# A decoder layer on one core: the fourth head's scores between two halves of the output projection, and unread matmuls in TensorE's waits

## The chip, the cores and the metric

The kernel runs on one core of a Trainium2 chip. The time is device microseconds (us) of one execution. A batch here means one of the 8 sequences, and a seam is the place where TensorE goes from one batch's last work to the next batch's.

## The reference, cut to what matters

For each of 8 sequences (512 tokens, 256 features, a context of 1024 tokens) the layer computes three blocks, each with a residual and a layer norm:

```python
x = layernorm(x + attn(x))            # convolution, position, qkv; 16 heads in bf16, 512 x 512 scores
y = causal_attention(x) + attention(x, ctx)     # 16 heads, fp32; 512 x 512 and 512 x 1024 scores
x = layernorm(x + y @ Wp + bp)
x = layernorm(x + routed_ffn(x))      # router, chosen expert, spline; then a norm of its own inside
```

The product `y @ Wp` of 512 x 256 by 256 x 256 in fp32 is the output projection of the title.

## The kernel before, in words

Five engines run hand-written streams that meet through semaphores. TensorE (PE) works its stream in order; nothing can be reordered by a scheduler.

A batch `b` on PE has two large stages. In the first, the heads stage, the 16 heads of the first attention are scored: `scores1(h)` writes four 128x512 tiles into banks 0 to 3 (line 1320), each after VectorE (DVE) has read the tile of the head before (semaphore `s1_evac`); `pv1(h)` multiplies by the values (line 1333). Heads 0 and 1 are scored at the end of the batch before (line 1304), so the loop at line 1394 begins with head 2, and "the fourth head" is `h == 3`. DVE scales every tile and takes its row minimum (line 768), ScalarE (ACT) takes the exponential (line 602), and both normalize (lines 961 and 612). In the second stage, 16 head groups of causal and cross attention are scored twice (lines 1501, 1505, 1540, 1543) and multiplied by the values (line 1558).

The seam carries the rest of the batch before (`c = b - 1`) between the heads of batch `b`:

- DVE ends batch `c` with `finish` (lines 1067 to 1073): `y_tmp`, which frees a slot (`slot_out`), then `y_sb` (`y_done`).
- PE waits for that slot, scores head 2, transposes `y_sb` (`heads_to_features`, line 1253), waits for ACT's copy `featA` (line 558), and runs the whole projection (`second_out`: `token_out` over 4 token tiles, line 1208, operands `wp_sb,featA`) into banks 5 and 6. `wp_mm` is raised once per two tiles.
- DVE's order is: norm of head 0, tiles of head 2, norm of head 1, tiles of head 3, then `second_residual` (lines 798, 773, 777: add banks 5 and 6 to `x_res`, sums of the norm), norm of head 2, `add_position` (line 752, writes `xs` of batch `b + 1`), tiles of head 4, `second_norm` (line 782, writes `r_sb`), norm of head 3, tiles of head 5.
- PE goes on with head 3, `position` (operands `xs,pe_sb`), head 4, then `first_qk` (`qk_sb,xs`), which waits for `add_position`, then head 5, `pv1(0)`, and the transposes of `r_sb`, whose copy `featB` ACT makes before its exponentials of head 5.

`keep_clock(at, n)` (line 1356) issues `n` bf16 matmuls of 128x512 into a bank that nobody reads; before the change it stands at the batch's end (4 of them) and four times later in the heads stage. `FILLERS` is 8. The last batch has no batch `b + 1` to prepare, and after it `tail` does the rest of the last sequence.

Of the kernel before, what the change touches and what calls it, by code (L numbers as in the profile page):

```python
# [37 lines left out]
def decoder_layer(nc, x, xT, ctxT, conv_w, peT, qkT, vT, outT, Wk, bk, Wq, bq, Wv, bv, Wck, bck, Wcq, bcq,  # L38
# [12 lines left out]
    NT = S // P  # L51
# [37 lines left out]
    FILLERS = 8  # L89
# [25 lines left out]
    with ctx:  # L115
        def sb(name, shape, dt=fp32):
            return ctx.enter_context(nc.sbuf_tensor(name, shape, dt))

        def sem(name):
            return ctx.enter_context(nc.semaphore(name))  # L120
# [8 lines left out]
        wp_sb = sb("wp_sb", [P, KD, D])  # L129
# [126 lines left out]
        out_mm, res_done, wp_mm = sem("out_mm"), sem("res_done"), sem("wp_mm")  # L256
        ln_stats, ln_var_in, ln_rstd, ln_done = ([sem(f"{n}{k}") for k in range(4)] for n in ("ln_stats", "ln_var", "ln_rstd", "ln_done"))
# [3 lines left out]
        slot_in, slot_out = sem("slot_in"), sem("slot_out")  # L261
# [103 lines left out]
        def uses_before(b, prev):  # L365
            return b * USES - FFN_USES if prev else 0
# [834 lines left out]
        def _(pe):  # L1201
# [3 lines left out]
            def project(dst, lhsT, rhs, tiles=KD):  # L1205

                for k in range(tiles):
                    last = mm(dst, lhsT(k), rhs(k), start=(k == 0), stop=(k == tiles - 1))  # L1208
                return last
# [12 lines left out]
            def position(b, m):  # L1222
                pe.wait_ge(conv_done, FIRST + b * KD + KD)
                project(bank[:, EXTRA_BANKS[m], :], lambda k: pe_sb[:, k, P * m:P * (m + 1)],
                        lambda k: xs[:, k, :]).then_inc(ex_mm, 1)

            def first_qk(b, i):

                if i == 0:
                    pe.wait_ge(ex_evac, (b + 1) * KD)  # L1230
                project(bank[:, EXTRA_BANKS[QK_AT[i]], :], lambda k: xs[:, k, P * i:P * (i + 1)], lambda k: qk_sb[:, k, :]).then_inc(ex_mm, 1)
# [7 lines left out]
                                       lambda k: v_sb[:, k, :])  # L1239
                    last.then_inc(ex_mm, 1)  # L1240

            def token_out(w, first_bank, done):

                for t in range(NT):
                    last = project(bank[:, first_bank + t // 2, D * (t % 2):D * (t % 2 + 1)], lambda k: featA[:, k, P * t:P * (t + 1)],
                                   lambda k: w[:, k, :])
                    if t % 2:
                        last.then_inc(done, 1)

            def to_features(src, first_bank, done):  # L1250
                for t in range(NT):
                    for k in range(KD):
                        last = nc.tensor.transpose(bank[:, first_bank + k, P * t:P * (t + 1)], src[:, t, P * k:P * (k + 1)], ident[:])
                last.then_inc(done, 1)

            def heads_to_features(c):
                pe.wait_ge(y_done, (c + 1) * HG)
                to_features(y_sb, 5, y_tr)

            def second_out(c):  # L1260
                pe.wait_ge(y_evac, c * 2 + 1)
                token_out(wp_sb, 5, wp_mm)

            def tokens_to_features(c):
                pe.wait_ge(ln_done[1], (c + 1) * NT)
                to_features(r_sb, 5, y_tr)

            def route(c):
                pe.wait_ge(y_evac, c * 2 + 2)
                for t in range(NT):  # L1270
                    last = project(bank[:, 7, ST * t:ST * (t + 1)], lambda k: featB[:, k, P * t:P * (t + 1)], lambda k: sigT[:, k, :])
                last.then_inc(route_mm, 1)

            def hidden_features(c):
                project(bank[0:HID, 5, :], lambda k: cw1_sb[:, k, :], lambda k: featB[:, k, :]).then_inc(gelu_in, 1)
# [36 lines left out]
            def batch(b, prev=True, ahead=True):  # L1312
                uses, base, c = all_uses[prev], uses_before(b, prev), b - 1

                def scores1(h):
                    i, rows = h // GH, slice(GW * (h % GH), GW * (h % GH + 1))
                    for t in range(NT):
                        n = NT * h + t
                        pe.wait_ge(s1_evac, b * H * NT + n - A1_BANKS + 1)
                        mm(bank[:, n % A1_BANKS, :], q_1[rows, i, P * t:P * (t + 1)], k_1[rows, i, :], start=True, stop=True,  # L1320
                           tile_position=(GW * (h % GH), 0)).then_inc(s1_mm, 1)

                def pv1(h):

                    if h < BY_DMA:
                        pe.wait_ge(p1T_in[h % E1_SLOTS], transposed(b, h))
                    else:
                        n = b * (H - BY_DMA) + h - BY_DMA
                        pe.wait_ge(tile_dve, n + 1)
                        pe.wait_ge(tile_act, n + 1)  # L1330
                    g = h // 2 % 4
                    for j in range(4):
                        last = mm(bank[GW * g:GW * (g + 1), PV1_BANKS[h // 8], :], v1[:, h, j, :], p1T[:, h % E1_SLOTS, :, j, :],  # L1333
                                  start=(h % 2 == 0 and j == 0), stop=(h % 2 == 1 and j == 3), tile_position=(0, GW * g))
                    last.then_inc(o1_mm, 1)
# [19 lines left out]
                    for _ in range(n):  # L1355
                        mm(bank[:, at, :], identb[:], k_1[:, 0, :], start=True, stop=True)

                if prev:
                    pe.wait_ge(slot_out, base)
                pe.wait_ge(qk_ready, (b + 1) * NT * 2)  # L1360
                pe.wait_ge(v1_ready, b * 16 + 16)
                def values(i):
                    if i == 0:
                        pe.wait_ge(ctx_in, b * 16 + 16)
                        if prev:
                            pe.wait_ge(tiles_in, b)
                        if ahead:
                            pe.wait_ge(qk_cast, (b + 1) * NT + 1)
                    else:
                        pe.wait_ge(vj_evac, b * PAIRS + i)  # L1370
                    if i == CTX_PAIRS and ahead:
                        pe.wait_ge(qk_cast, (b + 2) * NT)
                    if i == CTX_PAIRS + 1 and prev:
                        pe.wait_ge(spline_done, b)
                    for half in range(2):
                        dst = bank[:, 7 if i < CTX_PAIRS else VALUES_BANK, D * half:D * (half + 1)]
                        if i < CTX_PAIRS:
                            t = 2 * i + half
                            last = mm(dst, ctx_sb[:, P * t:P * (t + 1)], wcv_sb[:], start=True, stop=True)
                        else:  # L1380
                            t = 2 * (i - CTX_PAIRS) + half
                            last = project(dst, lambda k: featB[:, k, P * t:P * (t + 1)], lambda k: wv_sb[:, k, :])
                    last.then_inc(vj_mm, 1)
# [10 lines left out]
                for h in range(2, H):  # L1394
                    scores1(h)
                    if prev and h == 2:
                        heads_to_features(c)
                        second_out(c)
                    if h >= 5:
                        pv1(h - 5)  # L1400
                    if ahead and h == 3:
                        for m in range(KD):
                            position(b + 1, m)
                    if ahead and h == 4:
                        first_qk(b + 1, 0)
                        pe.wait_ge(ex_evac, (b + 2) * KD)
                    if prev:
                        if h == 5:
                            tokens_to_features(c)
                        if h == 6:  # L1410
                            if ahead:
                                pe.wait_ge(qk_cast, (b + 1) * NT + 1)
                            route(c)
                        if h == 7:
                            hidden_features(c)
                    if h in (8, 10, 12, 14):
                        values((h - 8) // 2)
                    if h in (9, 11, 13, 15):
                        context_key((h - 9) // 2)
                    if 9 <= h < 13:  # L1420
                        keep_clock(6, 4 if h % 2 else 2)
# [201 lines left out]
            def tail(c):  # L1623
                base = uses_before(c + 1, True)
                pe.wait_ge(slot_out, base)
                heads_to_features(c)
                second_out(c)
                tokens_to_features(c)
                route(c)
                hidden_features(c)  # L1630
                compressed(c)
                expert_columns(c, base, tail_uses)
                gather(c, base, tail_uses)
# [63 lines left out]
```

## Time and profile before

| what | us |
|---|---|
| runs | 2385.14, 2398.91, 2401.06 (median 2398.91) |
| the profiled execution | 2390.6 |
| its span | 2388.9 |
| TensorE busy | 2205.1 (92% of the span) |
| VectorE busy | 1876.4 (79%) |
| ScalarE busy | 1406.9 (59%) |

Matmul ends in the profile are modelled, so a busy PE is not PE at its peak. A row of the timeline merges neighbouring instructions of one kind; what stands in brackets is the idle time of the engine ahead of it and what ended that. The granted clock is given as a share of full speed: 1.00 is 2.4 GHz, 0.50 is 1.2 GHz.

### The profile page before, as it was taken

The page shows a single profiled execution, that of the slowest core. Times are in us where ns is not written, and L with a number is a line of the kernel's source. Part 1 is how long each engine was busy: PE and PEld are TensorE (multiplying, and loading weights), DVE is VectorE, ACT ScalarE, POOL GpSimd, SP SyncE. Part 2 cuts the span into 40 slices and gives each one's busy share as a digit, 9 for nine tenths or more (in the row PEclk, how much of TensorE's full clock was granted, in tenths as well). Part 3 has the DMA queues.
Part 4 walks back from the last instruction along what each step waited for, and adds up shares of the span by engine and source line. Part 5 has one row for each costly group of instructions (what it writes and reads, how often), then busy time and mean ns, then how long its engine had stood idle before and what let it go on. Part 6 is the DMA issues. An engine that isn't in the chain of part 4 may idle for free.

```text
span 2388.9 us, 37143 instructions
## 1 busy us (share of the span) xinstructions
PE 2205.1 (92%) x12850; PEld 1006.5 (42%) x12866; DVE 1876.4 (79%) x5149; ACT 1406.9 (59%) x2977; POOL 189.1 (8%) x349
## 2 busy tenths in 40 slices
PE   4999989999899998999989998999989999889992
PEld 1345433543345433454335443454334543345432
DVE  5868769788797879888698887988879786878854
ACT  2844678446764578546784466844677456754550
POOL 3011000100011000110001100010001100001000
PEclk8799999999999999999999998999989999789995
DMA  3600025000430006100160002500043000510000
GB/s 102 129 10 1 1 48 95 10 1 1 94 57 10 1 19 112 25 7 1 36 115 10 1 1 55 97 10 1 1 80 62 10 1 10 98 36 1 1 10 9
DMA packets 250843, 81.65 MB, mean 34 GB/s; under 512 B 236064, under 2 KB 247328, under 8 KB 250656
## 3 DMA queue, kind: packets, MB, share of 16 engines
q1 hardware_dynamic: 250656, 79.29, 16.3%
q8 instruction: 102, 1.67, 0.3%
q14 instruction: 85, 0.70, 0.1%
HBM read 16.35 MB, written 4.19 MB: 9 GB/s over the span
## 4 chain that ended last, share of the span: by engine, by line
PE 75%; ACT 11%; DVE 9%; issue 3%; DMA 1%; SPq 0%; POOL 0%; DVEq 0%; POOLq 0%; ACTq 0%
PE bank L1505 22%; PE bank L1558 13%; PE bank L1543 8%; PE bank L1208 7%; ACT work L602 6%; PE bank L1501 5%; PE bank L1460 4%; PE bank L1540 4%; DVE work L768 3%; PE bank L1333 2%; PE bank L1518 2%; ACT o1T L623 2%; PE bank L1320 1%; PE bank L1569 1%; ACT work L658 1%
## 5 line engine op out<-in xcount | busy, mean ns | idle before, releaser
L658 ACT ACTIVATE work<-bank 128x512 f32<-128x512 f32 (+3 forms) x1536 | 737.5, 553 | 561.6 <-PE bank L1543 287.2
L1037 DVE TENSOR_REDUCE top_half<-bank 128x1 f32<-128x512 f32 x1024 | 625.7, 682 | 24.1 <-PE bank L1505 24.1
L1505 PE MATMUL bank<-k_c,q_c 32*128 32x512 f32 x2048 | 630.7, 636 | 0.0
L1543 PE MATMUL bank<-q_c,k_c 32*128 32x512 f32 x2048 | 549.1, 629 | 0.0
L602 ACT ACTIVATE work<-work,neg 128x512 bf16<-128x512 bf16 x512 | 362.8, 718 | 60.7 <-DVE work L768 60.7
L768 DVE TENSOR_SCALAR_CACHE_REDUCE work<-bank 128x512 bf16<-128x512 f32 x512 | 322.4, 687 | 75.4 <-PE bank L1320 43.0
L1505 PEld LDWEIGHTS bank<-k_c,q_c 32*128 32x128 f32 x2048 | 274.5, 185 | 244.5 <-DVE top_half L1037 158.9
L1558 PE MATMUL bank<-work,v_flat 128*32 128x512 f32 (+3 forms) x3072 | 315.3, 545 | 9.2 <-ACT work L658 8.8
L1543 PEld LDWEIGHTS bank<-q_c,k_c 32*128 32x128 f32 x2048 | 227.0, 183 | 92.4 <-ACT work L658 57.2
L1034 DVE CUSTOM_DVE_ANT_0 masked<-bank,mask_w 128x384 bf16<-128x384 f32 (+3 forms) x512 | 223.1, 488 | 53.8 <-PE bank L1501 48.6
L1540 PE MATMUL bank<-q_s,k_s 32*128 32x512 f32 (+3 forms) x1024 | 259.1, 476 | 0.0
L1501 PE MATMUL bank<-k_s,q_s 32*128 32x128 f32 (+3 forms) x1024 | 198.5, 480 | 2.0 <-DVE top_s L1034 1.2
L1558 PEld LDWEIGHTS bank<-work,v_flat 128*32 128x32 f32 x3072 | 91.2, 109 | 234.4 <-issue 130.0
L1320 PE MATMUL bank<-k,q 32*128 32x512 bf16 x448 | 138.1, 401 | 26.6 <-DVE work L768 15.0
L1540 PEld LDWEIGHTS bank<-q_s,k_s 32*128 32x128 f32 x1024 | 141.6, 187 | 23.7 <-issue 8.9
L1333 PE MATMUL bank<-work,v 128*32 128x512 bf16 x512 | 145.2, 413 | 6.1 <-DMA work<-work 5.7
L1501 PEld LDWEIGHTS bank<-k_s,q_s 32*128 32x128 f32 x1024 | 102.9, 186 | 80.6 <-DVE top_s L1034 33.9
L517 POOL TENSOR_SCALAR ln_var<-mv 128x4 f32<-128x4 f32 x32 | 8.7, 272 | 1561.2 <-DVE mv L777 1561.2
L528 POOL TENSOR_SCALAR_AFFINE_SELECT work<-work 128x512 f32<-128x512 f32 x128 | 81.2, 634 | 602.8 <-ACT work L658 602.8
L1049 DVE COPY featA<-bank 128x512 f32<-128x512 f32 x64 | 44.3, 692 | 105.4 <-PE bank L1558 105.4
L961 DVE TENSOR_SCALAR work<-work,rden 128x512 bf16<-128x512 bf16 x424 | 123.0, 350 | 4.5
L602 ACT ACTIVATION_READ_ACCUMULATOR work<-work,neg 128x1 bf16 x512 | 102.3, 200 | 0.0
(191 smaller groups left out, 2260.4 us busy)
## 6 DMA issues: line engine op xcount, KB each, us to landing
xT_pad<-xT SPq DMA_DIRECT2D x16, 256.0 KB, 3.2
ctx_sb<-ctxT SPq DMA_DIRECT2D x8, 512.0 KB, 3.2
x_res<-x SPq DMA_DIRECT2D x8, 512.0 KB, 4.4
out<-r_sb SPq DMA_DIRECT2D x8, 512.0 KB, 3.1
work<-work SPq DMA_TRANSPOSE x112, 4.4
qk_sb<-qkT SPq DMA_DIRECT2D x1, 512.0 KB, 4.7
pe_sb<-peT SPq DMA_DIRECT2D x1, 256.0 KB, 4.4
v_sb<-vT SPq DMA_DIRECT2D x1, 256.0 KB, 5.5
```

Of the source, the lines that this page charges most:

```text
L602: nc.scalar.activation(e1[:, h % E1_SLOTS, t, :], s1[:, h % 2, t, :], ACT.Exp, bias=neg1[:, h % 2, t:t + 1], scale=-1.0, accum_out=den1[:, ...
L658: nc.scalar.activation(pT[:, s % PT_SLOTS, g, q0:S], exp_bank(n)[:, 0:S - q0], ACT.Exp, scale=SCALE).then_inc(pT_ready, 1)
L768: nc.vector.tensor_scalar(s1[:, h % 2, t, :], bank[:, (NT * h + t) % A1_BANKS, :], -SCALE, None, ALU.mult, ALU.min, accum_out=neg1[:, h % ...
L1034: nc.vector.tensor_tensor_reduce(masked[:, g, 0:n], scores[:, 0:n], mask_w[:, S - n:S], -1.0, -MASKED, ALU.add, ALU.min, top_s[:, i % 2, u ...
L1037: nc.vector.tensor_reduce(top_half[:, i % 2, g, u // 2, u % 2:u % 2 + 1], scores, AX.X, ALU.max, negate=True).then_inc(slot_out, 1)
L1208: last = mm(dst, lhsT(k), rhs(k), start=(k == 0), stop=(k == tiles - 1))
L1333: last = mm(bank[GW * g:GW * (g + 1), PV1_BANKS[h // 8], :], v1[:, h, j, :], p1T[:, h % E1_SLOTS, :, j, :], start=(h % 2 == 0 and j == 0), ...
L1501: mm(dst[:, 0:n], q_s[rows, i, P * u:n], k_s[rows, i, 0:n], start=True, stop=True, tile_position=(GW * g, 0)).then_inc(slot_in, 1)
L1505: mm(dst, q_c[rows, i, P * t:P * (t + 1)], k_c[rows, i, S * half:S * (half + 1)], start=True, stop=True, tile_position=(GW * g, 0)).then_i ...
L1540: mm(dst[:, 0:S - q0], k_s[rows, i, q0:q0 + P], q_s[rows, i, q0:S], start=True, stop=True, tile_position=(GW * g, 0)).then_inc(sT_mm, 1)
L1543: mm(dst, k_c[rows, i, P * u:P * (u + 1)], q_c[rows, i, :], start=True, stop=True, tile_position=(GW * g, 0)).then_inc(sT_mm, 1)
L1558: last = mm(dst[GW * g:GW * (g + 1), q0:S], v_flat[:, at:at + GW], pT[:, s % PT_SLOTS, g, q0:S], start=(s % BURST == 0), stop=(s % BURST = ...
```

## The change

Four edits, all on PE, all between the batches. The wait for `slot_out` moves from ahead of head 2 to behind it, with eight unread matmuls into bank 4 in between. Five more stand between the transposes of `y_sb` and the projection. The projection is cut in two: token tiles 0 and 1 ahead of `scores1(3)`, tiles 2 and 3 behind it. And where there is a next batch, eight unread matmuls into bank 6 stand ahead of `first_qk`, behind a wait until DVE has read bank 6 (`ln_stats[1]`). No other engine's stream is touched. The tail only calls the two halves one after the other.

```diff
-            def token_out(w, first_bank, done):
+            def token_out(w, first_bank, done, tiles):
-                for t in range(NT):
+                for t in tiles:
...
-            def second_out(c):
+            def second_out(c, half):
                 pe.wait_ge(y_evac, c * 2 + 1)
-                token_out(wp_sb, 5, wp_mm)
+                token_out(wp_sb, 5, wp_mm, range(2 * half, 2 * half + 2))
...
-                if prev:
-                    pe.wait_ge(slot_out, base)
                 pe.wait_ge(qk_ready, (b + 1) * NT * 2)
...
                 for h in range(2, H):
                     scores1(h)
                     if prev and h == 2:
+                        keep_clock(4, FILLERS)
+                        pe.wait_ge(slot_out, base)
                         heads_to_features(c)
-                        second_out(c)
+                        keep_clock(4, FILLERS // 2 + 1)
+                        second_out(c, 0)
+                    if prev and h == 3:
+                        second_out(c, 1)
                     if h >= 5:
                         pv1(h - 5)
                     if ahead and h == 3:
                         for m in range(KD):
                             position(b + 1, m)
                     if ahead and h == 4:
+                        if prev:
+                            pe.wait_ge(ln_stats[1], b * NT)
+                            keep_clock(6, FILLERS)
                         first_qk(b + 1, 0)
```

PE's stream at the first seam (batch 0 to batch 1), before the change, from the last transposes of batch 0 to the scores of head 5; `k,q` is a head's scoring, `k,identb` the unread matmuls:

```order
L1569 MATMUL bank<-ident,featA 128x128 x4
L1356 MATMUL bank<-k,identb 128x512 x4
L1320 MATMUL bank<-k,q 128x512 x4
L1253 MATMUL bank<-ident,y_sb 128x128 x8
L1208 MATMUL bank<-wp_sb,featA 128x256 x8
L1320 MATMUL bank<-k,q 128x512 x4
L1208 MATMUL bank<-xs,pe_sb 128x512 x4
L1320 MATMUL bank<-k,q 128x512 x4
L1208 MATMUL bank<-qk_sb,xs 128x512 x2
L1320 MATMUL bank<-k,q 128x512 x4
```

The same piece of PE's stream in the changed kernel, from the unread matmuls at the batch's end on:

```order
L1356 MATMUL bank<-k,identb 128x512 x4
L1320 MATMUL bank<-k,q 128x512 x4
L1356 MATMUL bank<-k,identb 128x512 x8
L1253 MATMUL bank<-ident,y_sb 128x128 x8
L1356 MATMUL bank<-k,identb 128x512 x5
L1208 MATMUL bank<-wp_sb,featA 128x256 x4
L1320 MATMUL bank<-k,q 128x512 x4
L1208 MATMUL bank<-wp_sb,featA 128x256 x4
L1208 MATMUL bank<-xs,pe_sb 128x512 x4
L1320 MATMUL bank<-k,q 128x512 x4
L1356 MATMUL bank<-k,identb 128x512 x8
L1208 MATMUL bank<-qk_sb,xs 128x512 x2
```

The scores of head 3 moved up past four of the projection's eight matmuls, and 21 unread matmuls came in at three places.

## Rows read from the trace of the kernel before

**Rows 1.** The page: span, TensorE's busy share, granted clock in 40 slices.
```profile
span 2388.9 us, 37143 instructions
PE 2205.1 (92%) x12850; PEld 1006.5 (42%) x12866; DVE 1876.4 (79%) x5149; ACT 1406.9 (59%) x2977; POOL 189.1 (8%) x349
PEclk8799999999999999999999998999989999789995
```

**Rows 2.** Chain that ended last, first seam: start us, us, what.
```profile
333.69 1.02 ACT featA L558
334.75 5.41 PE bank L1208 x16
...
348.58 3.63 PE bank L1208 x4
```

**Rows 3.** Timeline of PE, first seam: start us, us, group, idle before.
```profile
329.31 0.81 PE L1356 MATMUL bank<-k,identb 128*128 128x512 bf16 x3
331.59 1.03 PE L1320 MATMUL bank<-k,q 32*128 32x512 bf16 x4 [1.47 <-DVE y_tmp L1069]
332.56 1.09 PE L1253 MATMUL bank<-ident,y_sb 128*128 128x128 f32 x8
334.75 5.41 PE L1208 MATMUL bank<-wp_sb,featA 128*128 128x256 f32 x16 [1.10 <-ACT featA L558]
340.09 1.03 PE L1320 MATMUL bank<-k,q 32*128 32x512 bf16 x4
341.05 3.70 PE L1208 MATMUL bank<-xs,pe_sb 128*128 128x512 f32 x8
...
348.58 3.63 PE L1208 MATMUL bank<-qk_sb,xs 128*128 128x512 f32 x4 [2.87 <-DVE xs L752]
352.15 1.03 PE L1320 MATMUL bank<-k,q 32*128 32x512 bf16 x4
```

**Rows 4.** Timeline of DVE and ACT, first seam.
```profile
330.21 0.69 DVE L768 TENSOR_SCALAR_CACHE_REDUCE work<-bank 128x512 bf16<-128x512 f32 x1
...
331.57 0.42 DVE L1073 TENSOR_TENSOR y_sb<-y_sb,y_tmp 128x256 f32<-128x256 f32 x1
...
335.56 0.88 DVE L961 TENSOR_SCALAR work<-work,rden 128x512 bf16<-128x512 bf16 x3
...
340.51 0.69 DVE L768 TENSOR_SCALAR_CACHE_REDUCE work<-bank 128x512 bf16<-128x512 f32 x1 [4.07 <-PE bank L1320]
...
347.25 1.28 DVE L752 TENSOR_TENSOR xs<-bank,xs 128x512 f32<-128x512 f32 x2
...
353.30 0.69 DVE L768 TENSOR_SCALAR_CACHE_REDUCE work<-bank 128x512 bf16<-128x512 f32 x1
...
355.21 1.01 ACT L558 COPY featB<-bank 128x1024 f32<-128x1024 f32 x1 [1.51 <-PE bank L1253]
```

**Rows 5.** PE by stretches: from:to us, busy (count), granted clock, DMA share, GB/s.
```profile
334.88:338.29 3.41, 3.41 (x9) 0.50 0.68 122
...
348.53:351.95 3.42, 3.37 (x4) 0.50 0.81 153
...
1765.06:1775.30 10.24, 9.14 (x20) 0.50 0.57 104
```

**Rows 6.** Timeline, DVE's first tile of head 3 at later seams; PE's projection at the sixth.
```profile
623.85 0.69 DVE L768 TENSOR_SCALAR_CACHE_REDUCE work<-bank 128x512 bf16<-128x512 f32 x1 [5.07 <-PE bank L1320]
...
1475.88 0.69 DVE L768 TENSOR_SCALAR_CACHE_REDUCE work<-bank 128x512 bf16<-128x512 f32 x1 [5.40 <-PE bank L1320]
...
1758.09 0.69 DVE L768 TENSOR_SCALAR_CACHE_REDUCE work<-bank 128x512 bf16<-128x512 f32 x1 [2.39 <-PE bank L1320]
...
2043.61 0.69 DVE L768 TENSOR_SCALAR_CACHE_REDUCE work<-bank 128x512 bf16<-128x512 f32 x1 [4.07 <-PE bank L1320]
...
1754.01 3.72 PE L1208 MATMUL bank<-wp_sb,featA 128*128 128x256 f32 x16 [1.10 <-ACT featA L558]
```

**Rows 7.** Timeline of DVE behind the sixth seam's `first_qk`.
```profile
1775.81 0.69 DVE L768 TENSOR_SCALAR_CACHE_REDUCE work<-bank 128x512 bf16<-128x512 f32 x1 [1.40 <-PE bank L1320]
...
1779.36 0.18 DVE L954 RECIPROCAL rden<-den 128x4 f32<-128x4 bf16 x1 [1.02 <-ACT work L602]
```

More of the change, by code:

```diff
@@ L1626, in tail @@
                 heads_to_features(c)
-                second_out(c)
+                second_out(c, 0)
+                second_out(c, 1)
                 tokens_to_features(c)
```

## The prediction

> **What bounds the kernel now.** First the page. TensorE is busy for 92% of the span and DVE for 79%, so neither share alone says who is waited for at a seam; the clock line shows that TensorE's granted clock dips in nearly every batch [rows 1]. Then the chain that ended last, cut to the first seam: it leaves DVE and runs through ACT's copy `featA` (1.02 us) and the whole projection (5.41 us), and later through `first_qk` (3.63 us) [rows 2]. Then the timeline of PE there. It waits 1.47 us for `y_tmp`, 1.10 us for `featA`, and 2.87 us for `xs` [rows 3]. The stretches show what the waits cost beyond themselves: from 334.88 to 338.29, just where the projection begins, and from 348.53 to 351.95, just where `first_qk` begins, the granted clock is 0.50, that is 1.2 GHz [rows 5]. The same projection took 3.72 us at the sixth seam, where the clock was not low, against 5.41 here [rows 3, 6].
>
> Who pays for it? DVE. It ends the norm of head 1 at 335.56 + 0.88 = 336.44, and its next work, the first tile of head 3, begins at 340.51, after 4.07 us of idle time that PE's scores of head 3 end [rows 4]; these stand behind the whole projection. From there DVE has no gap until after 353.30, the first tile of head 5: residual, norm sums, `add_position` at 347.25, head 4, `r_sb` all stand back to back [rows 4]. So a microsecond taken out of that 4.07 us moves the rest of the seam by one. PE's 2.87 us wait for `xs` and ACT's 1.51 us wait before `featB` [rows 3, 4] are consequences of DVE's lateness and not separate gains. The seven seams (batches 0 to 1 up to 6 to 7) have DVE waits of 4.07, three times 5.07, 5.40, 2.39 and 4.07 us [rows 4, 6].
>
> **The slot wait moved, and the first eight unread matmuls.** Removing the wait lets head 2's scores begin when the fillers at the batch's end are over (329.31 + 0.81 = 330.12) rather than at 331.59 [rows 3]. But its last tile needs DVE's last tile of head 1, over at 330.21 + 0.69 = 330.90 [rows 4], so it issues at about 331.0 and PE is free at about 331.2. DVE gains nothing from this: it reads head 2 only after `finish` and a norm. Three unread matmuls show 0.81 us; with the modelled end of the last taken off (1.03 us for four scores that stand 0.97 apart from what follows, 331.59 to 332.56 [rows 3]) one costs about 0.22. Eight are 1.75 us, until 332.9. `y_sb` is done at 331.57 + 0.42 = 331.99 [rows 4], and the transposes began at 332.56. They now begin about 0.35 us later: this is the one cost on the path of edit one. Its bounds: 0 if the fillers run faster than thought, 1.9 us more if the clock is low there and each takes 0.43.
>
> The Trainium skill, page "TensorE: Matmul & The Clock Gate", section "The mechanism" of its Part 3, says that matmuls keep their program order in start and end; only weight loads are pulled ahead. That speaks against this edit, for the eight cannot be overtaken by the transposes that are ready before them. Were it otherwise, the 0.35 would be nothing and the sum about 2.5 us better over seven seams. No row here shows a matmul overtaking another.
>
> **The five unread matmuls.** They cost 5 x 0.22 = 1.1 us and stand in a wait of 1.10 us [rows 3]. I take nothing. The cover is ACT's copy; were it gone, 1.1 us a seam.
>
> **The cut projection.** `featA` is copied 0.35 us later, so the first half begins at 334.75 + 0.35 = 335.1. At full clock the whole takes 3.72 [rows 6], a half 1.8. Head 3's scores then issue at 336.9 and the first tile lands 0.4 us later (340.09 to 340.51 before [rows 3, 4]), at 337.3. DVE is ready at 336.44, so its wait shrinks from 4.07 to about 0.9 us. That is 3.2 us at the first seam. The second half runs from 337.9 to 339.7, under the four tiles that DVE reads (337.3 to 339.75); the residual's second add needs it only after that. Positions follow (3.70 us [rows 3]) until 343.3; `add_position` now stands at 347.25 - 3.2 = 344.05 and still finds them done, by 0.7 us. So nothing is late next on DVE. By the same end state (a wait of 0.9), the seams gain 3.2, 3 x 4.2, 4.5, 1.5 and 3.2: together 25.0 us.
>
> **The eight ahead of `first_qk`.** Head 4's scores end at 344.3, the sums they wait for are long made. They run until 346.0, while `xs` is there at 345.3: `first_qk` starts 0.7 us late. It then takes about 1.9 us at full clock (the eight records of `xs,pe_sb` take 3.70, these are four) instead of 3.63. Head 5's scores come at 347.8 instead of 352.15 [rows 3], and DVE does not want them before 353.30 - 3.2 = 350.1. So the edit is hidden twice over at the first seam and worth nothing there. At the sixth seam the clock stayed low for 10.24 us from `first_qk` on [rows 5], and DVE then waited 1.40 us for PE and 1.02 for ACT [rows 7]: 2.4 us that this edit removes. Sum: 25.0 + 2.4 = 27.4 us.
>
> From the profiled execution's 2390.6 us this gives 2363. It lies 8.3 us under the median of the runs, and the runs differ by 16 us among themselves; I carry the gain over to the median: 2398.9 - 27.4 = 2371.5, rounded to 2372.
>
> The tail and the other stages are as before. The second stage shifts with the seam: everything there waits on PE, ACT and DVE work that itself moves.
>
> **The rivals.**
>
> *The order works, the clock does not.* If the unread matmuls do not keep the clock up, the half projection takes about twice 1.8. DVE's first tile of head 3 comes at 335.1 + 3.7 + 0.4 = 339.2, a gain of 1.3 us against 340.51. Over seven seams: about 10 us, 2389. For it speaks that the four fillers at the batch's end did not prevent the dip at 334.88. Against it: between those four and the dip lay two waits of 1.47 and 1.10 us, and now no idle microsecond is left between 329.3 and the projection.
>
> *The dip moves behind `first_qk`.* PE reaches head 5 early and then waits for `r_sb` (done at about 349.1) and for DVE's tiles of head 5 (from 350.8): a microsecond or so of gaps with scores, value products and transposes and no large matmul before the router. If the clock falls there, it costs what it cost at the sixth seam, 2.4 us [rows 7], at the six seams that have a next batch: 27.4 - 14.4 = 13 us, 2386. Against it: before, head 5 to the second `pv1` hold the same work, tighter packed, and the rows after 351.95 are at full rate again [rows 3, 5]. The Trainium skill, same page, section "Part 4: PE-mode transpose", says that transposes do not count as busy for the clock as matmuls do. That makes this rival likelier, and no row here tests it alone; by that rule the time is this rival's.
>
> *Slower: fillers at the low clock.* If the clock is at 0.50 when PE reaches the eight, they take 3.4 us and not 1.75, and the five take 2.2 against a wait of 1.1. The transposes start 2.0 us late, take about 0.9 more, the five add 1.0, and the cold half 3.7. DVE's tile then comes at 334.75 + 2.0 + 0.9 + 1.0 + 3.7 + 0.4 = 342.8, that is 2.3 us later than before; with 1.4 from the eight ahead of `first_qk` up to 3.7 a seam, 26 us in all, 2425. It decides from the point where more than about half of the seams enter the fillers cold. Against it: at the first seam the rows before the dip are at full rate (1.03 for four scores, 1.09 for the transposes [rows 3]).
>
> *Given back downstream.* Later waits of the heads stage (PE for ACT's `k_c`, the transposing DMAs) and clock dips that fall elsewhere take most of it: some 8 us left, 2391. I see no queue that does not shift with the seam, but the executions before already spread by 16 us.
>
> **How the numbers follow.** Chances: the forecast 0.57, with a range of its own from 2360 to 2382; order without clock 0.16; dip moved 0.13; given back 0.09; slower 0.05. A difference of 1% (24 us) is about what a measurement of this kernel can tell from no change; the bound lies at 2375, just above my value. Of the forecast I put 0.50 beyond it and 0.07 short; the other cases are within 1% but for the slow one. The range 2358 to 2392 holds the forecast, the two partial cases and most of the fourth, and leaves out the slow case and edges.
>
> **What would show it right or wrong.** Right: the page's clock above 0.94; the projection in two rows of about 1.9 us each with the head 3 scores between; DVE's wait before head 3 near 0.9 us at all seven seams; PE's waits of 1.10 and 2.87 us filled by rows of line 1356; the distance on DVE from `y_sb` (331.57) to head 5 (353.30) down from 21.7 to 18.5 us. Wrong: a granted clock of 0.50 over the first half (second case), or over the router's matmuls (third), or a DVE wait for PE at head 4, 5 or 6 that was not there. The forecast fails altogether if DVE's 4.07 us wait reappears whole in front of some later instruction.

## The result and the profile after

| | before | after |
|---|---|---|
| median of 4 runs, us | 2397.15 | 2364.05 |
| lowest to highest, us | 2385.14 to 2401.06 | 2359.54 to 2370.91 |
| the profiled execution | 2390.6 | 2362.12 |
| its span | 2388.9 | 2360.3 |

The ratio is 0.9871 with a 95% interval from 0.9833 to 0.9908: 1.3% faster. Before the fourth run of before came in, its median was the 2398.91 of the table ahead.

The page of the changed kernel: span, busy shares, granted clock in 40 slices.

```profile
span 2360.3 us, 37437 instructions
PE 2204.1 (93%) x13005; PEld 1008.7 (43%) x13005; DVE 1874.3 (79%) x5149; ACT 1406.3 (60%) x2977; POOL 189.0 (8%) x349
PEclk8899999999999999999999998999999999989995
```

TensorE's busy time is the same although it has 139 unread matmuls more (21 at six seams, 13 at the last), since many others ran at the higher clock: the mean granted clock of the span rose from 0.940 to 0.955 ([rows 1] has the clock line of before).

PE's timeline at the first seam after the change (start us, us, group, idle before):

```profile
326.29 1.90 PE L1356 MATMUL bank<-k,identb 128*128 128x512 bf16 x8
328.03 1.04 PE L1253 MATMUL bank<-ident,y_sb 128*128 128x128 f32 x8
328.90 1.24 PE L1356 MATMUL bank<-k,identb 128*128 128x512 bf16 x5
330.17 1.99 PE L1208 MATMUL bank<-wp_sb,featA 128*128 128x256 f32 x8
332.09 1.03 PE L1320 MATMUL bank<-k,q 32*128 32x512 bf16 x4
333.06 1.99 PE L1208 MATMUL bank<-wp_sb,featA 128*128 128x256 f32 x8
334.89 3.60 PE L1208 MATMUL bank<-xs,pe_sb 128*128 128x512 f32 x8
...
341.12 1.88 PE L1208 MATMUL bank<-qk_sb,xs 128*128 128x512 f32 x4
342.93 1.03 PE L1320 MATMUL bank<-k,q 32*128 32x512 bf16 x4
```

These answer [rows 3]. No row has an idle time in brackets any more; the projection is two rows of 1.99 us, and `first_qk` takes 1.88 us where it took 3.63. DVE at the same seam, `y_sb`, the first tile of head 3 and `add_position`:

```profile
326.58 0.42 DVE L1073 TENSOR_TENSOR y_sb<-y_sb,y_tmp 128x256 f32<-128x256 f32 x1
...
332.52 0.69 DVE L768 TENSOR_SCALAR_CACHE_REDUCE work<-bank 128x512 bf16<-128x512 f32 x1 [1.07 <-PE bank L1320]
...
339.25 1.28 DVE L752 TENSOR_TENSOR xs<-bank,xs 128x512 f32<-128x512 f32 x2
```

The wait of 4.07 us in [rows 4] is 1.07 now, and `add_position` stands 12.67 us behind `y_sb` where it stood 15.68.

Where the 28.6 us of span went is read by cutting both traces at the last `y_sb` of each batch and at the first projection of the second stage (`unit(0)`, operand `wq_sb`), which is behind the heads stage:

| seam | DVE's wait before head 3, before / after | `y_sb` to `unit(0)`, before / after | gain |
|---|---|---|---|
| 1 | 4.07 / 1.07 | 84.22 / 79.95 | 4.3 |
| 2 | 5.07 / 1.07 | 85.22 / 81.03 | 4.2 |
| 3 | 5.07 / 1.07 | 85.16 / 79.95 | 5.2 |
| 4 | 5.07 / 1.06 | 85.25 / 80.65 | 4.6 |
| 5 | 5.40 / 3.03 | 87.08 / 86.51 | 0.6 |
| 6 | 2.39 / 1.07 | 85.22 / 81.21 | 4.0 |
| 7 | 4.07 / 1.07 | 89.00 / 81.56 | 7.4 |

The last column sums to 30.3 us; the waits of the second column, before less after, sum to 21.7. The rest of the batches, `unit(0)` to the next `y_sb`, got 6.8 us longer in all, with 74 us of low clock in them where before had 58; the tail is the same. And 5.0 us lie ahead of the first seam, in code that the change does not touch: that part is the spread between executions.

At seams 2 to 4 four microseconds of the wait went and not three. There the clock had fallen to 1.2 GHz before the change already at the transposes of `y_sb`, one group earlier than in [rows 3] (1.97 us where the first seam has 1.09), so the projection had begun 0.9 to 1.0 us later:

```profile
614.95 1.97 PE L1253 MATMUL bank<-ident,y_sb 128*128 128x128 f32 x8
```

Seam 5 is the exception. Its rows on PE, and the granted clock of two stretches there (from:to us, busy, clock, DMA share, GB/s):

```profile
1443.53 1.91 PE L1356 MATMUL bank<-k,identb 128*128 128x512 bf16 x4
...
1446.39 1.90 PE L1356 MATMUL bank<-k,identb 128*128 128x512 bf16 x8
...
1450.27 1.99 PE L1208 MATMUL bank<-wp_sb,featA 128*128 128x256 f32 x8
...
1469.27 3.59 PE L1208 MATMUL bank<-sigT,featB 128*128 128x72 f32 x16
```

```profile
1438.50:1445.30 6.80, 6.80 (x28) 0.51 0.00 0
1469.30:1479.60 10.30, 10.30 (x29) 0.51 0.78 164
```

The clock was at 1.2 GHz already when PE came to the fillers at the end of the batch (four in 1.91 us, against 0.81 for three in [rows 3]), so PE left its batch late, and everything up to the projection was two microseconds late. The eight fillers behind head 2 and the projection itself were at the full rate again. Then the clock was low once more from the matmuls of the router on (the product that chooses the expert, `sigT,featB`: 3.59 us, at the other seams 2.00), for some 10 us, and DVE waited 1.05 us before head 7. The wait before head 3 explains 2.0 of the 6.6 us by which `unit(0)` is later here than at seam 1; the other 4.6 lie behind the start of the router.

### The profile page after: what moved, and what is told of

Same layout as the page of the kernel before. It is cut to its first block, busy times and chain, and to the rows that moved or that the text cites. A ratio compares the mean times of both kernels' runs of the same rounds, so it can differ in the third digit from the quotient of the medians.

```text
span 2360.3 us, 37437 instructions
## 1 busy us (share of the span) xinstructions
PE 2204.1 (93%) x13005; PEld 1008.7 (43%) x13005; DVE 1874.3 (79%) x5149; ACT 1406.3 (60%) x2977; POOL 189.0 (8%) x349
## 4 chain that ended last, share of the span: by engine, by line
PE 76%; ACT 12%; DVE 8%; issue 3%; DMA 1%; POOL 0%; SPq 0%; DVEq 0%; POOLq 0%; ACTq 0%
PE bank L1511 22%; PE bank L1564 13%; PE bank L1549 8%; PE bank L1208 7%; ACT work L602 7%; PE bank L1507 5%; PE bank L1466 4%; PE bank L1546 4%; DVE work L768 3%; PE bank L1333 2%; PE bank L1575 2%; PE bank L1524 2%; ACT o1T L623 2%; PE bank L1320 1%; PE bank L1356 1%
## 5 line engine op out<-in xcount | busy, mean ns | idle before, releaser
L1564 PE MATMUL bank<-work,v_flat 128*32 128x512 f32 (+3 forms) x3072 | 320.2, 552 | 9.2 <-ACT work L658 8.8
L1333 PE MATMUL bank<-work,v 128*32 128x512 bf16 x512 | 138.8, 398 | 15.3 <-DMA work<-work 15.3
```

What stands on the lines that cost most here:

```text
L1564: last = mm(dst[GW * g:GW * (g + 1), q0:S], v_flat[:, at:at + GW], pT[:, s % PT_SLOTS, g, q0:S], start=(s % BURST == 0), stop=(s % BURST = ...
```

## The experiments

All runs of a kernel are compared with before on the same chip; the medians of before there were 2390.54 (e1 to e4), 2386.87 (e5, e8 to e10) and 2389.35 us (e11, e12, e6, e7). The changed kernel's 2364.05 belongs to a before of 2397.15, so two kernels with different medians of before are compared by their ratios; the changed kernel's is 0.9871 (0.9833 to 0.9908). The traces decide more than the medians here, since before itself spreads over 11 to 18 us. In the fences, line 1320 becomes 1324 where two statements were added.

### The parts alone, and one part doubled

**e1_order_only**, the two moves without an unread matmul:

```diff
-                        keep_clock(4, FILLERS)
                         pe.wait_ge(slot_out, base)
                         heads_to_features(c)
-                        keep_clock(4, FILLERS // 2 + 1)
                         second_out(c, 0)
...
-                            keep_clock(6, FILLERS)
```

> The cut projection and the moved slot wait alone, without any of the 21 unread matmuls. Theory 1 (order and clock share the gain): the transposes of y_sb begin some 0.9 us sooner than in the changed kernel, but the granted clock falls to 0.50 at the first half of the projection as before, which then takes about 3.7 us and not 1.99; DVE's wait before head 3 is about 2 us against 4.07 to 5.07 before and 1.07 after; some 14 to 16 us gained, time near 2382. Rival (order is all): the clock does not fall or its fall is harmless, time near the changed kernel's 2364 or under it.

Measured: 2395.06 us against 2390.54, ratio 1.0009 (0.9988 to 1.003). No gain at all. Yet the first part went as theory 1 says. PE at the first seam, and DVE:

```profile
332.95 3.48 PE L1208 MATMUL bank<-wp_sb,featA 128*128 128x256 f32 x8 [1.10 <-ACT featA L558]
...
353.59 3.56 PE L1208 MATMUL bank<-sigT,featB 128*128 128x72 f32 x16
```

```profile
336.93 0.69 DVE L768 TENSOR_SCALAR_CACHE_REDUCE work<-bank 128x512 bf16<-128x512 f32 x1 [1.85 <-PE bank L1320]
...
357.72 0.69 DVE L768 TENSOR_SCALAR_CACHE_REDUCE work<-bank 128x512 bf16<-128x512 f32 x1 [1.03 <-PE bank L1320]
```

The wait before head 3 is 1.85 us, 2.2 less than before, with the first half of the projection at the low clock. But the router is now at the low clock too (3.56 us), DVE waits again at head 7, whose scores stand behind the router, and `unit(0)` comes 85.35 us behind `y_sb`: later than before the change (84.22). The router was at the low clock at six seams of seven (3.40 to 3.69 us). Theory 1 had the wait right and the time 13 us too low, since both theories missed this; it is the second rival of the prediction, in a kernel that I had not asked it of.

**e2_fill_only**, all fillers, the projection whole ahead of head 3:

```diff
                         second_out(c, 0)
-                    if prev and h == 3:
                         second_out(c, 1)
```

> All unread matmuls and the moved slot wait stay, the projection is whole again ahead of head 3. Theory 1: it runs at full clock in 3.7 us, DVE's wait before head 3 is about 1.07 + 1.8 = 2.9 us at each seam, 7 x 1.8 = 12 to 13 us behind the changed kernel: near 2377. Rival (order is all): the fillers bring nothing, time near 2397.

Measured: 2406.06 us, ratio 1.0064 (1.004 to 1.0089), slower than before. DVE's wait before head 3 is 2.79 us at each seam, as theory 1 said; the projection takes 3.72 us. But the router takes 3.69 us at all seven seams, and the kernel is 29 us above the 2377 of theory 1.

**e4_first16**, sixteen unread matmuls behind head 2:

```diff
-                        keep_clock(4, FILLERS)
+                        keep_clock(4, 2 * FILLERS)
```

> Sixteen unread matmuls instead of eight behind head 2. Theory 1 (they stand on the path, since the transposes cannot pass them): eight more are 1.74 us more; DVE's wait before head 3 grows from 1.07 to about 2.8 at every seam, 12 us in all, near 2376. Rival (they are hidden by DVE's own work, or buy more clock than they cost): time within 3 us of 2364.

Measured: 2403.06 us, ratio 1.0049 (1.0029 to 1.0069). The wait grew by 1.72 us to 2.79 at each seam: the fillers do stand on the path, and the transposes of `y_sb` did not pass them, although `y_sb` was done (at 332.16 us, and they began at 334.91). Seven times 1.72 is 12 us. The kernel is 39 us slower than the changed one (1.8% by the ratios). PE and DVE at its first seam, and the clock behind the router's start:

```profile
356.54 3.69 PE L1208 MATMUL bank<-sigT,featB 128*128 128x72 f32 x16
```

```profile
360.80 0.69 DVE L768 TENSOR_SCALAR_CACHE_REDUCE work<-bank 128x512 bf16<-128x512 f32 x1 [1.63 <-PE bank L1320]
```

```profile
355.10:365.30 10.20, 10.20 (x31) 0.52 0.82 175
```

`unit(0)` is 86.2 to 87.2 us behind `y_sb` at every seam, against 79.95 to 81.6 at six of the changed kernel's.

**e3_no_last8**, without the eight ahead of `first_qk` (and the wait on `ln_stats[1]` left in place):

```diff
-                            keep_clock(6, FILLERS)
```

> Only the eight unread matmuls ahead of first_qk (and their wait) are gone. Theory 1 (hidden except where the clock then stays low): the granted clock falls to 0.50 at first_qk again, which takes 3.6 us; the distance from y_sb to DVE's first tile of head 5 does not change at most seams; 0 to 4 us behind the changed kernel. Rival: they hold up the clock for the router and the heads behind, and each seam loses 1 to 2.5 us, 2371 to 2380.

Measured: 2371.40 us, ratio 0.9914 (0.9892 to 0.9935). The clock did not fall at `first_qk`, which took 1.95 us; theory 1 had expected it to fall. PE's wait there is now 1.23 us where it was 2.87. The time is at the lower end of the rival's range, and by its mechanism: of seven seams two, the second and the sixth, have the router at the low clock. The routers of the first and the second seam, then `first_qk` and the router of the second and the third:

```profile
346.32 2.00 PE L1208 MATMUL bank<-sigT,featB 128*128 128x72 f32 x16
```

```profile
617.81 1.95 PE L1208 MATMUL bank<-qk_sb,xs 128*128 128x512 f32 x4 [1.23 <-DVE xs L752]
626.30 3.22 PE L1208 MATMUL bank<-sigT,featB 128*128 128x72 f32 x16
```

```profile
904.25 1.96 PE L1208 MATMUL bank<-qk_sb,xs 128*128 128x512 f32 x4 [1.24 <-DVE xs L752]
912.75 2.00 PE L1208 MATMUL bank<-sigT,featB 128*128 128x72 f32 x16
```

From `y_sb` to the router all three stand at the same distances from their `y_sb` (323.72, 603.70 and 890.15) within 0.01 us. The second fell to the low clock and lost 5.2 us to `unit(0)` (84.98 against 79.75 at the third and 79.71 at the first); the others did not. The third had a low stretch that ended 3.9 us ahead of its `y_sb`, the second had none there. The first had none either: its matmuls stand where the second's stand, within 0.01 us, from 160 us ahead of `y_sb` on, and the granted clock of both is 1.00 over all of that, up to the router. So neither the order of the instructions, nor their distances, nor the clock before decides it; with this stretch as it is, the seam is open to either.

### Is it the router stretch?

The expectations from here on weigh two theories, written for e5 below. Theory A: what is left of the path up to head 3 decides the time. Theory B: whether the granted clock is low over the router decides it.

Between `first_qk` and the router PE has head 5, `pv1(0)`, the transposes of `r_sb`, head 6, whose last three tiles wait 0.23 us each for DVE, and `pv1(1)`, and no large matmul. The next kernels put two unread matmuls ahead of each tile of head 6, in bank 7, once ACT has read it. The wait for ACT stood ahead of the router and stands ahead of head 6 now:

```diff
+                    if prev and ahead and h == 6:
+                        pe.wait_ge(qk_cast, (b + 1) * NT + 1)
                     for t in range(NT):
                         n = NT * h + t
+                        if prev and h == 6:
+                            keep_clock(7, 2)
```

**e8_first16_head6** adds this to e4:

> As with sixteen unread matmuls behind head 2 (2403 us), and in addition two unread matmuls into bank 7 ahead of each of head 6's four score tiles, where PE waited 0.23 us a tile for DVE. Theory B: the low stretch over the router is what cost 26 us beyond the 12 of the eight matmuls; the eight small fillers keep the clock up there, the router's matmuls take 2.0 and not 3.69 us, unit0 comes about 81.7 us behind y_sb and not 86.3, and the time is near 2376. Rival (the sixteen cost by themselves, by standing on the path or by delaying something else): the time stays within 5 us of 2403.

Measured: 2381.11 us, where e4 had 2403.06. The first seam's router, and the clock in the same stretch as above (its `y_sb` stands 1.5 us earlier):

```profile
355.55 2.00 PE L1208 MATMUL bank<-sigT,featB 128*128 128x72 f32 x16
```

```profile
355.10:365.30 10.20, 10.20 (x48) 1.00 0.83 165
```

1.00 against 0.52, and the router at 2.00 us at all seven seams. Eight matmuls more on TensorE at each seam took 22 us off (0.8% by the ratios; in the traces the seven seams from `y_sb` to `unit(0)` are 22.7 us shorter). Theory B holds: the low stretch over the router was the larger part of what sixteen fillers cost. The time is 5 us above the expected one, with one seam (the second) where PE was two microseconds late at the projection, as at seam 5 of the changed kernel, and a last one at 85.3.

**e11_order_head6** adds it to e1, with none of the change's own 21:

> The cut projection and the moved slot wait with none of the change's 21 unread matmuls (2395 us alone), plus the eight in head 6. Theory B: the projection's first half still runs into the low clock (3.5 us, DVE's wait 1.85), but the router no longer does (2.0 and not 3.6 us), unit0 comes about 81.5 us behind y_sb and not 85.8; about 4 us at six seams, near 2371. Rival (the order alone is worth nothing whatever the clock): 2390 or more.

Measured: 2365.65 us, ratio 0.9899 (0.9873 to 0.9925), where e1 had 2395.06. The router at the first seam, and DVE there, head 3 and head 7:

```profile
352.81 2.00 PE L1208 MATMUL bank<-sigT,featB 128*128 128x72 f32 x16
```

```profile
335.19 0.69 DVE L768 TENSOR_SCALAR_CACHE_REDUCE work<-bank 128x512 bf16<-128x512 f32 x1 [1.81 <-PE bank L1324]
...
355.17 0.69 DVE L768 TENSOR_SCALAR_CACHE_REDUCE work<-bank 128x512 bf16<-128x512 f32 x1 [0.22 <-PE bank L1324]
```

The projection's half is still at the low clock (3.34 to 3.59 us), the wait still 1.8, the router at 2.00 us at all seven seams, and the interval overlaps the changed kernel's. So the new order with the router at the full clock is worth 1.0%, against the 1.3% of the whole change; and what the change's fillers chiefly bought is not at the places where they stand. No run put head 6's fillers into the kernel before; its router was at the full clock at six seams of seven already.

Nor is it that PE only comes to the router at another moment. The fillers in head 6 make it about 1 us later, but the routers of e11 stand 24.3 to 24.6 us behind `y_sb` and none is low, while those of e1 (23.3 to 23.6 us at the six low ones) and of e4 (24.7 to 25.3 us) are.

**e9_head6** adds it to the changed kernel:

> The changed kernel with two unread matmuls ahead of each of head 6's four score tiles. Theory B: the one seam of seven with a low router (1444.71) is mended, 4 to 6 us gained, near 2359; the first wait stays 1.07. Rival (fillers there are in the way): PE is 0.3 to 1 us later at each router, 2364 to 2370.

Measured: 2362.66 us, ratio 0.9893 (0.9868 to 0.9918). No low router at any seam, and `unit(0)` at 80.65 to 81.21 us at all seven. But the good seams, 79.95 to 81.6 in the changed kernel, lost up to 0.7 of it, for the fillers put PE 1.0 us later at the router (23.59 us behind `y_sb`, not 22.60). The sum is no measurable gain over the changed kernel (0.9893 against 0.9871): both sides were partly right.

### How many fillers at the projection?

**e5_first4**, four instead of eight behind head 2:

```diff
-                        keep_clock(4, FILLERS)
+                        keep_clock(4, FILLERS // 2)
```

> Four unread matmuls instead of eight behind head 2, the rest as in the changed kernel. Theory A (what is left of the path): the transposes of y_sb begin 0.87 us sooner, DVE's wait before head 3 falls from 1.07 to about 0.2, 6 us in all, near 2359. Theory B (the granted clock behind the seam decides): the 0.87 us is gained, but whether the stretch of 1.2 GHz of some 10 us falls on the router, as it did at every seam with 16 matmuls there and at none but one in the changed kernel, follows from the moment at which PE gets there; if it does, each seam loses about 6 us to unit0 and the time is 2380 to 2400.

Measured: 2360.79 us, ratio 0.9888 (0.9864 to 0.9913). DVE's wait fell to 0.21 us at six seams, as theory A says. The first and the second seam show both outcomes:

```profile
336.13 0.69 DVE L768 TENSOR_SCALAR_CACHE_REDUCE work<-bank 128x512 bf16<-128x512 f32 x1 [0.22 <-PE bank L1320]
```

```profile
632.21 3.69 PE L1208 MATMUL bank<-sigT,featB 128*128 128x72 f32 x16
```

`unit(0)` is at 79.13 us behind the first `y_sb` and at 84.48 behind the second. Three seams of seven went the second way, and took back most of what the four fillers gave: the waits before head 3 sum to 7.7 us less than in the changed kernel, `y_sb` to `unit(0)` to 1.4 us less.

**e6_no_first8** and **e7_no_five** are the changed kernel without `keep_clock(4, FILLERS)`, and without `keep_clock(4, FILLERS // 2 + 1)`:

> The changed kernel without the eight behind head 2; the five ahead of the projection and the eight ahead of first_qk stay. Theory A: the transposes of y_sb begin as early as with four (the projection 2.74 us behind y_sb), so what four cost is nothing. If the five alone do not hold the clock, the first half takes 3.5 us as with order alone and DVE's wait is 1.8; if they do, it is 1.99 and the wait 0.2.

> The changed kernel without the five ahead of the projection. If the eight behind head 2 hold the clock alone, the first half still takes 1.99 us and DVE's wait stays 1.07; if not, 3.5 us and about 2.7.

Measured: 2366.77 and 2360.72 us, single runs. In both the half projection takes 1.99 us at all seven seams; the wait is 0.21 us at six seams with the five alone, and 1.06 with the eight alone. Either group holds the clock at the projection, and the other adds nothing there. At the router, e6 was low at two seams (second and seventh: `unit(0)` at 85.69 against 79.1 at the first), e7 at none. In e7 the row of the projection has its wait back, and the full rate all the same:

```profile
335.45 1.99 PE L1208 MATMUL bank<-wp_sb,featA 128*128 128x256 f32 x8 [1.10 <-ACT featA L558]
```

### The best of both

**e10_first4_head6** is e5 with the fillers in head 6:

> Four matmuls behind head 2 and the fillers in head 6 together. Theory B: both gains, DVE's wait 0.2 and no low router, 2353 to 2358. Rival: the fewer matmuls behind head 2 let the clock fall at the projection (its first half takes 3.5 us), then 2370 or more.

Measured: 2357.77 us, ratio 0.9874 (0.9854 to 0.9893). No low router; the wait 0.21 us at six seams.

**e12_first4_head6_no_last8** drops the eight ahead of `first_qk` as well:

> Four matmuls behind head 2, five ahead of the projection, eight in head 6, and none ahead of first_qk. Theory B: the ones ahead of first_qk are hidden and, with head 6's in place, not needed for the clock: 2355 to 2361, as with them. Rival (they carry the clock over the 1.2 us wait into head 5 and 6): the low stretch comes back over the router at some seams, 2365 to 2375.

Measured: 2355.40 us, ratio 0.9854 (0.9825 to 0.9883), the fastest median of the study. At two seams the clock now does fall at `first_qk`, and DVE pays 1.5 us at head 7, much less than a low router takes:

```profile
344.37 3.55 PE L1208 MATMUL bank<-qk_sb,xs 128*128 128x512 f32 x4 [1.24 <-DVE xs L752]
```

```profile
357.50 0.69 DVE L768 TENSOR_SCALAR_CACHE_REDUCE work<-bank 128x512 bf16<-128x512 f32 x1 [1.52 <-PE bank L1324]
```

Its interval overlaps those of e10 and of the changed kernel, whose ratio of 0.9871 is within it, so that it beats the changed kernel is not shown.

## Why the prediction was right, and where it was not

**The sum.** Forecast 2372 (2358 to 2392), measured 2364.05. The forecast gain was 27.4 us, the difference of medians 33.1, of spans 28.6. Of the 28.6, 5.0 lie ahead of the first seam, so that what the edits gave between these two executions is 23.6, under the forecast; and the median of before that the gain was taken from lay 8 us above the profiled execution. That 2364 lies under 2372 is spread as much as it is gain.

**The path.** That DVE's wait before head 3 is the one to watch, and that the rest of the seam follows it, held: the wait shrank and `add_position` moved up by the same 3.0 us. The wait came out at 1.07 us at six seams, forecast 0.9. The terms: the projection began 3.59 us behind `y_sb` where it was 3.18, so 0.41 late and not 0.35; the half took 1.92 us up to the next group, not 1.8. The distance from `y_sb` to head 5 on DVE is 18.7 us, forecast 18.5.

**The fillers on the path.** Eight cost 1.74 us (326.29 to 328.03), forecast 1.75; e4 confirmed the price with 1.72 more. The working did not give that price: 0.06 us taken off three in 0.81 leaves 0.25 each, and eight would be 2.0. The modelled end of this kind is longer, 0.16 us (a row of 1.90 for 1.74). The bound of 1.9 us for a low clock should have been 1.7, by the prediction's own 3.4 less 1.75. The Trainium skill, page "TensorE: Matmul & The Clock Gate", section "The mechanism" of its Part 3, has matmuls in program order; e4 agrees, with its 1.72 us.

**The eight ahead of `first_qk`.** "Hidden twice over" held: `first_qk` came 0.4 us later than in e3 (14.54 against 14.10 us behind `y_sb`) with no effect on DVE. That they were what brings `first_qk` to the full clock does not hold: in e3 it took 1.95 us without them, behind a wait that had shrunk to 1.23 us. At the sixth seam 4.0 us were gained, 1.3 by the wait and 2.7 behind it, forecast 1.5 and 2.4.

**The sum was near for partly other reasons.** Forecast by the waits was 25.0; they gave 21.7, because the fifth seam kept 3.03 us. Behind the waits I counted 2.4 us; there were 8.6 over the seven seams, with 1.8 lost at the fifth. Half of them, 4.4, are the last seam, where I had taken nothing but the wait. The low stretch of before

```profile
2048.37:2072.26 23.89, 21.13 (x54) 0.50 0.60 124
```

shrank to 6.8 us, and its router takes 2.00 us and not 3.69. At the first and third seams a low stretch at the context keys, which before stood 61 and 62 us behind those `y_sb`, is gone, and `unit(0)` is another 1.2 us earlier. Then 6.8 us were given back in the second stage, less than the 19 of the "given back" rival. So the forecast had the path right at six seams, and its sum came near because gains and losses that it had not counted nearly cancelled; that part was luck.

**The rivals.** The first, order works but clock does not: e1 shows its mechanism. Priced with the eight fillers, it had DVE's tile at 339.2, a wait of 2.8 us; without them the projection starts 0.85 us sooner, and the wait is 1.85. The changed kernel did not go that way. The third, slower by fillers at the low clock, did not happen, not even at the fifth seam: the eight took 1.74 us there and the projection's half 1.99, and its wait of 3.03 us, two more than at the others, came from a low clock at the end of the batch before. The second was the important one, and it was mis-sized. I priced a low stretch behind `first_qk` at 2.4 us a seam from [rows 7]. Measured up to `unit(0)`, a low router costs 5.2 us (e3, second seam), 5.4 (e5, second seam; its fifth 4.5) and 6.6 (e6, second seam). With the term as measured the rival would have stood at 2372 + 6 x 5.3 = 2404 and not at 2386, on the slower side. e2 with 2406 and e4 with 2403 lie there, though at seven seams and with 12 us of longer waits before head 3. The row I took it from ended its low stretch at 1775.30, ahead of the router; one that begins at the router covers the router, head 7 and the products behind it, where PE's rows have no gap to take it up. The profiled execution of the changed kernel met it at one seam of seven, so the forecast's choice stands; but of the seven kernels near it e1, e2 and e4 met it at six or seven seams, e3, e5 and e6 at two or three, and e7 at none, so 0.13 was little for a rival this near. How many seams fell in the other three executions no trace shows; the slowest, 2370.91 us, had a mean granted clock of 0.946 against 0.954 and 0.955.

**What decides the router.** Over the changed kernel and e1 to e7, 28 of 56 seams had the router at 3.2 us or more; over the five kernels with fillers in head 6, none of 35. So in this kernel the clock could fall over a stretch of scores, value products and transposes with gaps of 0.23 us, and with eight 128x512 matmuls inside it it did not. The Trainium skill, same page, "Part 4: PE-mode transpose", says that transposes do not count as busy for the clock in the way of matmuls; that is in line with it, but no run took only the transposes away. What makes one seam fall and its twin not, as in e3, stays open: the traces show equal work at equal distances and only another moment of the run. Why the order alone brings the router to the low clock at six seams, where it was low at one before, stays open with it. So it stays open, too, why the changed kernel met a low router at one seam only while e4 met it at seven; that the eight fillers are the right number is not shown, and e5, e6 and e7 speak against a special one.

## What to carry to other kernels

Price a wait of TensorE by what comes after it: here 1 to 3 us of waiting put matmuls of 2 us at half speed somewhere later, and the stretch that lost most was not the one that waited longest. When the order or the fillers change, look at the next stretch without large matmuls too, since its clock can fall though nothing in it was touched, as with the order alone (no gain, and 29 us less with eight fillers a seam in that stretch). Put fillers where TensorE already waits for another engine, and count them: the five in the wait of 1.10 us were free (without them, in e7, the projection begins at the same 3.59 us behind `y_sb`), while ahead of something that was ready each cost 0.22 us a seam.

## What the runs showed of the hardware that was not expected

- The granted clock fell behind short waits. At the first seam of before it fell behind waits of 1.47 and 1.10 us with scores and transposes between them [rows 3], at seams 2 to 4 already behind the one of 1.47 us. A wait of 1.23 us ahead of `first_qk` in e3 did not bring it down at any seam, and one of 1.23 to 1.24 us in e12 did at two seams and not at the others. The same wait can go either way.
- Two instruction streams equal within 0.01 us for 180 us, with a granted clock of 1.00 ahead of both, got 1.00 and 0.52 over the router and what follows (e3, first and second seam, 346.4 to 356.6 and 626.4 to 636.6 us).
- Once low at the router, the clock stayed there for some 10 us, through head 7 and the products behind it, although TensorE is shown busy without a gap in that stretch (10.20 of 10.20 us in e4).
